# Clamping the chunk sum for the growth factor on ScalarE instead of GpSimd, in a selective state-space block

## The chip, the cores and the metric

The kernel runs on one core of a Trainium2 chip. The metric is the device time of one execution in microseconds (us). Engines are named as in the profile: PE is TensorE's matmul side and PEld its weight loads, DVE is VectorE, ACT is ScalarE, POOL is GpSimd, SP is SyncE, which issues the DMAs.

## The reference, cut to what matters

The input is 8 sequences of 1024 tokens with 512 channels. A layer norm, a Mamba block (1024 inner channels, 16 states per channel, chunks of 128 tokens), a residual, a second layer norm, a product with int8 values and a residual follow one another. The part that the change touches is the scan inside a chunk:

```
A_bar = exp(d_c[..., None] * A)                       # A = -a < 0, one per state
BX = d_c[..., None] * B_c[:, :, None, :] * x_c[..., None]
log_A_cum = cumsum(log(maximum(A_bar, EPS)), axis=1)  # EPS = 1e-10
A_cum = exp(minimum(log_A_cum, 80))
wcum = cumsum(BX / maximum(A_cum_shifted, EPS), axis=1)
h = A_cum * wcum / maximum(A_bar, EPS) + h0 * A_cum
y = einsum('bls,blds->bld', C_c, h) + D * x_c
```

For each state the kernel needs 1 / maximum(A_cum_shifted, EPS), which it calls the growth. With total = the sum of d_c over the earlier tokens of the chunk, the growth is exp(a * min(total, ln(1e10) / a)), which is the same as exp(min(a * total, ln(1e10))).

## The kernel before, in words

A tile is one chunk of 128 tokens (in the partitions) by 1024 channels; there are 64 tiles. For one parity of the tile number two tiles are in flight, so every large buffer of a tile exists twice. The program is written as one instruction stream per engine, by hand: a function `whole` calls for each engine `start`, then `body(tile)` for every tile (a loop over pairs of tiles from tile 4 on, the last pair written out) and `end`. Semaphores that only count up order the engines; every `wait_ge` in the listing is such a wait.

`body` runs over 16 slots, one per state s. In slot s

- PE makes `cum` for slot s+2 (L961: the sum over earlier tokens of `step`, two PSUM buffers), then pieces of the next tile's front (input projection L866, transposes L850, the small projection L879, `total` L895) and of the previous tile's end (transposes L928, output projection L936, int8 product L951), then `state` for slot s (L971: the sum of `source`, one PSUM buffer).
- DVE makes `term` of slot s-1 (L1311: state times decay times C), `source` of slot s+1 (L1298: growth times B times delta times x), adds term s-1 to `acc` (L1321), then its pieces of front and end: the convolution taps (L1159 in slot 5, L1167 in slots 6 and 7), dt (L1191, slot 9), the softplus (L1196, L1201, L1203, slots 10 and 11), `delta` (L1213, slot 12), `dx` (L1222, slot 13), the correction of the last token (L1248, slot 6), the second norm's output `xn` (L1277) with its largest value and scale (L1279 to L1283, slot 15).
- ACT makes `decay` of slot s+2 (L699: exp(-a * cum)) and then `growth` of slot s+2 (L704: exp(a * room), written over `cum` in PSUM), with evacuations of PSUM banks and pieces of the front between them: the small projection `proj` in slot 9 (L568), then in slot 10 abs, exp, relu and ln of the softplus (L631, L635, L637, L641) and one `xc` evacuation, in slot 11 the other `xc` evacuation and the square (L648). At the end of slot 8 it runs two SiLUs (L620, L611) between two table loads (L620, L795). PE's front uses a single PSUM bank, `fbank`, so each front product or transpose waits until ACT has emptied the bank. At the start of slot 0 ACT waits for DVE's scale and quantizes (L685, L687).
- POOL makes `step` of slot s+3 (L463: delta clamped to [0, ln(1e10)/a]; waits until `cum` of slot s+1 is complete, since it has two buffers) and then `room` of slot s+2 (L473: total clamped likewise; one buffer, so it waits for the growth of slot s+1). In slot 14 it also makes `skip` of the next tile (L450: D times x, the start value of `acc`), which waits only for pieces of the front that are done by slot 11.

Slots above 15 belong to the next tile: `step` of the next tile's states 0, 1 and 2 is issued in slots 13, 14 and 15, `room` of its states 0 and 1 in slots 14 and 15. In the source the order of POOL is

```
limit_step(s + 3); limit_sum(s + 2); if s == 0: finish(prev); if s == 14: skip(nxt)
```

and that of ACT in slot 9 to 11 (slot numbers of the scan in brackets)

```
9:  decay(11), proj, growth(11)
10: abs, decay(12), exp, relu, growth(12), xc0, ln
11: decay(13), xc1, square, growth(13)
```

Of the kernel before, what the change touches and what calls it, by code (L numbers as in the profile page):

```python
# [9 lines left out]
ALU = mybir.AluOpType  # L10
ACT = mybir.ActivationFunctionType
AX = mybir.AxisListType

P = 128
BATCH, SEQ, D = 8, 1024, 512
DI = 1024
NS = 16
# [10 lines left out]
FIRST_PARTS = 8  # L28
EPS = 1e-10
LN_EPS = float(np.log(np.float32(EPS)))  # L30
NORM_EPS = 1e-5
INT8_MAX = 127.0
ROUND = 12582912.0
# [18 lines left out]
FRONT_ACT = ("xi0", "xi1", "xiT0", "tap3a", "xiT1", "tap3b", "z0", "xcT", "proj", "abs", "exp", "over", "xc0",  # L52
             "ln", "xc1", "square", "z1", "total0", "total1", "ct")
# [29 lines left out]
def at(steps, tile, name):  # L83

    return tile.n * len(steps) + steps.index(name) + 1


def slot_at(tile, slot):

    return tile.n * NS + slot + 1  # L90
# [7 lines left out]
def before(tile, slot, by):  # L98

    return (tile, slot - by) if slot >= by else (tile.shift(-1), NS - by + slot)  # L100


def mamba_block(nc, x, w_in, conv_w, conv_b, w_x, dt_w, dt_b, a_log, d_skip, w_out, rhs_t, out):
    with ExitStack() as ctx:
        def sb(name, shape, dt=F32):
            return ctx.enter_context(nc.sbuf_tensor(name, shape, dt))
# [4 lines left out]
        def sem(name):  # L111
            return ctx.enter_context(nc.semaphore(name))
# [10 lines left out]
        neg_a = sb("neg_a", [P, NS])  # L123
        pos_a = sb("pos_a", [P, NS])
        limit = sb("limit", [P, NS])
# [9 lines left out]
        rscale = sb("rscale", [P, D])  # L135
        rcol = sb("rcol", [P, KD])
        rinv = sb("rinv", [P, KD])
        curve = sb("curve", [P, 6])
        square_bias, below, above, ln_join, round_up, round_back = (curve[:, i:i + 1] for i in range(6))


        xt = sb("xt", [P, D])
# [18 lines left out]
        total = sb("total", [P, DI])  # L161
# [5 lines left out]
        room = sb("room", [P, DI])  # L167
# [40 lines left out]
        cum = [ps(f"cum{i}", [P, DI]) for i in range(2)]  # L208
# [17 lines left out]
        front_act = sem("front_act")  # L226
# [7 lines left out]
        step_ready = sem("step_ready")  # L234
        room_ready = sem("room_ready")
        cum_ready = sem("cum_ready")
        growth_ready = sem("growth_ready")
# [34 lines left out]
        def stand(eng):  # L272

            eng.sem_inc(stood, 1)
# [139 lines left out]
        def _(pool):  # L414
# [3 lines left out]
            nc.gpsimd.memset(hfirst[:, :], 0.0)  # L418
            nc.gpsimd.memset(last_marks[:, :], 0.0)
            for column, value in ((square_bias, SQUARE_BIAS), (below, -JOIN), (above, 1.0 + JOIN), (ln_join, 0.0),  # L420
                                  (round_up, ROUND), (round_back, -ROUND)):
                nc.gpsimd.memset(column, value)
            for h in halo:
                nc.gpsimd.memset(h[:, :, :], 0.0)
# [38 lines left out]
                nc.gpsimd.tensor_scalar(step[s % 2][:, :], delta[t.parity][:, :], limit[:, s:s + 1], 0.0,  # L463
                                        ALU.min, ALU.max).then_inc(step_ready, 1)

            def limit_sum(t, s):
                if s == 0:
                    pool.wait_ge(front_act, at(FRONT_ACT, t, "total1"))
                user, old = before(t, s, 1)
                if user is not None:  # L470
                    pool.wait_ge(growth_ready, slot_at(user, old))
                stand(pool)
                nc.gpsimd.tensor_scalar(room[:, :], total[:, :], limit[:, s:s + 1], 0.0,  # L473
                                        ALU.min, ALU.max).then_inc(room_ready, 1)

            def finish(t):
                with pool.If(other_carries(pool, t)):
                    a = acc[t.parity][:, :]
                    if isinstance(t.n, int) and t.n == TILES - 1:
                        pool.wait_ge(room_ready, slot_at(t, NS - 1))  # L480
                    else:
                        pool.wait_ge(front_dve, at(FRONT_DVE, t.shift(1), "delta"))
                        pool.wait_ge(room_ready, slot_at(t.shift(1), 2))
                    stand(pool)
                    nc.gpsimd.memset(hcarry, 0.0).then_inc(carry_cleared, 1)
                    pool.wait_ge(carry_cleared, t.n + 1)
                    pool.wait_ge(added, slot_at(t, NS - 1))
                    for s in range(1, NS):
                        pool.wait_ge(carry_terms, carry_at(t, s))
                        if s > 1:  # L490
                            pool.wait_ge(carry_added, carry_at(t, s - 1))
                        stand(pool)
                        nc.gpsimd.tensor_tensor(a, a, carried[:, :], ALU.add).then_inc(carry_added, 1)
                    pool.wait_ge(carry_saved, 16 * carry_at(t))
                    pool.wait_ge(last_saved[0], ring_at(t, NS - 2))
                    pool.wait_ge(last_saved[1], ring_at(t, NS - 1))
                    pool.wait_ge(carry_added, carry_at(t))
                    stand(pool)
                    nc.gpsimd.tensor_tensor(hmain[t.parity], hmain[t.parity], hcarry, ALU.add).then_inc(carry_merged, 1)
                    pool.wait_ge(carry_merged, t.n + 1)  # L500
                with pool.Else():
                    skip_carries(pool, t, carry_added)
                    if not (isinstance(t.n, int) and t.n == 0):
                        pool.wait_ge(carry_merged, t.n)
                    pool.sem_inc(carry_cleared, 1)
                    pool.sem_inc(carry_merged, 1)

            def start():
                t = Tile(0, 0)
                skip(t)  # L510
                for s in range(3):
                    limit_step(t, s)
                for s in range(2):
                    limit_sum(t, s)

            def body(t, more, more2):
                prev, nxt = t.shift(-1), t.shift(1)
                for s in range(NS):
                    if s + 3 < NS:
                        limit_step(t, s + 3)  # L520
                    elif more:
                        limit_step(nxt, s + 3 - NS)
                    if s + 2 < NS:
                        limit_sum(t, s + 2)
                    elif more:
                        limit_sum(nxt, s + 2 - NS)
                    if s == 0 and prev is not None:
                        finish(prev)
                    if more:
                        if s == 14:  # L530
                            skip(nxt)
# [4 lines left out]
        def _(act):  # L536
# [157 lines left out]
            def decays(t, s):  # L694
                act.wait_ge(cum_ready, slot_at(t, s))
                user, old = before(t, s, 4)
                if user is not None:
                    act.wait_ge(term_ready, slot_at(user, old))
                nc.scalar.activation(decay[s % 4][:, :], cum[s % 2][:, :], ACT.Exp, scale=neg_a[:, s:s + 1]).then_inc(decay_ready, 1)  # L699

            def growths(t, s):
                act.wait_ge(decay_ready, slot_at(t, s))
                act.wait_ge(room_ready, slot_at(t, s))
                nc.scalar.activation(cum[s % 2][:, :], room[:, :], ACT.Exp, scale=pos_a[:, s:s + 1]).then_inc(growth_ready, 1)  # L704

            def finish(t):
                with act.If(other_carries(act, t)):
# [6 lines left out]
            def start():  # L714
                t = Tile(0, 0)
                norm_guess(t)
                norm_xnT(t)
                front_xi(t, 0)
                front_xi(t, 1)
                front_xiT(t, 0)  # L720
                front_tap3(t, 0)
                front_xiT(t, 1)
                front_tap3(t, 1)
                front_gate(t, 0)
                front_xcT(t)
                nc.scalar.preload_act_table_set(EXP_AND_LN)
                front_proj(t)
                front_abs(t)
                front_over(t)
                front_xc(t, 0)  # L730
                front_log(t)
                front_xc(t, 1)
                front_square(t)
                front_gate(t, 1)
                front_total(t, 0)
                front_total(t, 1)
                front_ct(t)
                norm_guess(t.shift(1))
                norm_xnT(t.shift(1))
                decay_once(t)  # L740
                for s in range(2):
                    decays(t, s)
                    growths(t, s)

            def body(t, more, more2):
                prev, nxt = t.shift(-1), t.shift(1)
                prev2 = prev.shift(-1) if prev is not None else None
                for s in range(NS):
                    ahead, slot = (t, s + 2) if s + 2 < NS else (nxt, s + 2 - NS)
                    if s == 0 and prev2 is not None:  # L750
                        end_q(prev2)
                    if s == 10 and more:
                        front_abs(nxt)
                    if more or s + 2 < NS:
                        decays(ahead, slot)

                    if s == 0 and prev is not None:
# [333 lines left out]
        def _(dve):  # L1091
# [17 lines left out]
            done(nc.vector.reciprocal(limit[:, :], pos_a[:, :]), limit_ready, 1)  # L1109
            nc.vector.tensor_scalar(limit[:, :], limit[:, :], -LN_EPS, None, ALU.mult).then_inc(limit_ready, 1)  # L1110
            nc.vector.tensor_scalar(neg_a[:, :], pos_a[:, :], -1.0, None, ALU.mult).then_inc(consts_dve, 1)
# [356 lines left out]
```

## Time and profile before

| | |
|---|---|
| runs | 6188.1, 6189.16, 6192.53 us; median 6189.16 us |
| profiled execution | 6189.9 us from its first to its last instruction; the page gives no time outside this span |
| mean granted TensorE clock | 0.989 of full speed |
| PE / DVE / ACT / POOL busy | 92% / 91% / 60% / 44% of the span |
| instructions that the change touches | 1024 `room` on POOL (L473), 1024 `growth` on ACT (L704) |

The busy share of an engine is the union of its instructions over the whole span. The timeline rows give the start in us from the beginning of the span, the duration, the engine, the line in the kernel, the operation, what it writes and reads, and, in square brackets, how long the engine had been idle before it and who ended that idle time. Instructions of one engine overlap a little: the pitch from start to start is shorter than the duration. A row with "x8" stands for eight in a row.

### The profile page before, as it was taken

Reading aid. Unit: us, or ns where it says so; the run is one execution under the profiler, and the core shown is the slowest. Engines: PE = TensorE matmul, PEld = TensorE weight load, DVE = VectorE, ACT = ScalarE, POOL = GpSimd, SP = SyncE. Lnnn points to the kernel's source line nnn. Section 1 sums busy time; section 2 is a strip of 40 time slices with the busy share of each in tenths; the row PEclk is TensorE's granted clock in tenths of the full one; section 3 lists DMA queues with packets and bytes.
Section 4 is the critical chain, followed back from the end, with each engine's and each line's share of the span. In section 5 each row is a group of like instructions: output and inputs, shape, how many; then the busy total and the mean of one; then the engine's idle time right before and its main releaser. Section 6 shows DMA issues by size and latency. Waiting matters only on the chain.

```text
span 6189.9 us, 77161 instructions
## 1 busy us (share of the span) xinstructions
PE 5686.4 (92%) x16152; PEld 2632.6 (43%) x16152; DVE 5633.4 (91%) x7057; ACT 3734.6 (60%) x4618; POOL 2744.1 (44%) x2138
## 2 busy tenths in 40 slices
PE   5999999999999999999999999999999999999997
PEld 2444444444444444444444444444444444444443
DVE  4999999999999999999999999999999999999997
ACT  3666665665666666656666666566566666665664
POOL 2444444444444444444444444444444444444443
PEclk9999999999999999999999999999999999999998
DMA  1121121121111211211212112112121121121120
GB/s 64 11 17 19 14 17 15 14 19 13 16 18 14 17 16 14 19 15 14 19 13 17 16 14 19 15 14 19 13 16 18 14 17 15 14 19 15 14 17 11
DMA packets 157893, 104.23 MB, mean 17 GB/s; under 512 B 121008, under 2 KB 121008, under 8 KB 157488
## 3 DMA queue, kind: packets, MB, share of 16 engines
q1 hardware_dynamic: 157488, 100.71, 17.8%
q14 instruction: 380, 3.11, 0.2%
q8 instruction: 25, 0.41, 0.0%
HBM read 42.63 MB, written 16.78 MB: 10 GB/s over the span
## 4 chain that ended last, share of the span: by engine, by line
PE 37%; DVE 31%; issue 20%; ACT 3%; DVEq 2%; ACTq 0%; DMA 0%; SPq 0%
PE state L971 13%; DVE acc L1321 11%; PE cum L961 10%; DVE term L1311 6%; PE fbank L866 5%; DVE conv L1167 4%; DVE conv L1159 2%; PE ebank L936 2%; PE ebank L916 2%; PE fbank L879 2%; DVE xn L1277 1%; ACT xiT L568 1%; DVE dx L1222 1%; DVE delta L1213 1%; PE fbank L850 1%
## 5 line engine op out<-in xcount | busy, mean ns | idle before, releaser
L699 ACT ACTIVATE decay<-cum,neg_a 128x1024 f32<-128x1024 f32 x1024 | 1138.6, 1112 | 1944.8 <-PE cum L961 1942.4
L971 PE MATMUL state<-sources,tri_upto 128*128 128x512 f32 x4096 | 1980.6, 606 | 187.4 <-DVE term L1311 187.1
L473 POOL TENSOR_SCALAR room<-total,limit 128x1024 f32<-128x1024 f32 x1024 | 1352.8, 1321 | 1653.9 <-ACT cum L704 1448.2
L463 POOL TENSOR_SCALAR step<-delta,limit 128x1024 f32<-128x1024 f32 x1024 | 1243.4, 1214 | 1661.2 <-PE cum L961 1038.5
L961 PE MATMUL cum<-step,tri_before 128*128 128x512 f32 x4096 | 1940.7, 596 | 3.5 <-DVE sources L1298 3.5
L1311 DVE SCALAR_TENSOR_TENSOR term<-state,crow,decay 128x1024 f32<-128x1024 f32 x1024 | 1308.8, 1278 | 247.4 <-PE state L971 135.9
L1321 DVE TENSOR_TENSOR acc<-acc,term 128x1024 f32<-128x1024 f32 x1024 | 1459.2, 1425 | 0.2
L1298 DVE SCALAR_TENSOR_TENSOR sources<-cum,brow,dx 128x1024 f32<-128x1024 f32 x1024 | 1303.1, 1273 | 12.1 <-ACT cum L704 12.1
L971 PEld LDWEIGHTS state<-sources,tri_upto 128*128 128x128 f32 x4096 | 744.5, 191 | 1068.5 <-issue 941.7
L961 PEld LDWEIGHTS cum<-step,tri_before 128*128 128x128 f32 x4096 | 777.7, 192 | 941.7 <-issue 935.6
L704 ACT ACTIVATE cum<-room,pos_a 128x1024 f32<-128x1024 f32 x1024 | 1143.6, 1117 | 17.6 <-POOL room L473 2.7
L866 PE MATMUL fbank<-win,xnT 128*128 128x512 f32 x2048 | 983.3, 603 | 113.4 <-ACT xiT L568 109.4
L866 PEld LDWEIGHTS fbank<-win,xnT 128*128 128x128 f32 x2048 | 376.5, 191 | 573.9 <-issue 423.4
L936 PE MATMUL ebank<-wout,ygT 128*128 128x512 f32 x1024 | 484.0, 596 | 0.5 <-DVE ygT L1248 0.5
L936 PEld LDWEIGHTS ebank<-wout,ygT 128*128 128x128 f32 x1024 | 190.8, 191 | 217.3 <-issue 202.1
L1167 DVE SCALAR_TENSOR_TENSOR conv<-xiT,cw,conv 128x128 f32<-128x128 f32 x1024 | 279.4, 334 | 0.2
L597 ACT ACTIVATE conv<-xiT,cb,cw 128x128 f32<-128x128 f32 x512 | 210.1, 489 | 0.1
L1159 DVE SCALAR_TENSOR_TENSOR conv<-xiT,cw,conv 128x128 f32<-128x128 f32 x512 | 189.7, 440 | 18.3 <-ACT conv L597 18.3
L1201 DVE SCALAR_TENSOR_TENSOR xi<-acc,xi 128x1024 f32<-128x1024 f32 x64 | 78.4, 1225 | 131.4 <-ACT acc L648 131.4
L450 POOL TENSOR_TENSOR acc<-xiT,dskip 128x1024 f32<-128x1024 f32 x64 | 151.9, 2374 | 78.7 <-DVE xi L1201 78.7
L685 ACT ACTIVATE xn<-xn,curve,esmall 128x512 f32<-128x512 f32 x64 | 52.1, 813 | 213.8 <-DVE esmall L1283 213.8
L895 PE MATMUL fbank<-delta,tri_before 128*128 128x512 f32 x256 | 137.3, 618 | 20.8 <-ACT total L568 19.8
(125 smaller groups left out, 3972.7 us busy)
## 6 DMA issues: line engine op xcount, KB each, us to landing
hfirst<-hrows SPq DMA_DIRECT2D x496, 64.0 KB, 3.9
xt<-in_x SPq DMA_DIRECT2D x64, 256.0 KB, 2.6
hrows<-term SPq DMA_DIRECT2D x1024, 4.0 KB, 1.7
xres<-in_x SPq DMA_DIRECT2D x64, 256.0 KB, 2.7
out_x<-xres SPq DMA_DIRECT2D x64, 256.0 KB, 2.1
gate_last<-gate SPq DMA_DIRECT2D x512, 0.5 KB, 2.1
win<-in_w_in SPq DMA_DIRECT2D x2, 2048.0 KB, 10.7
hrows<-hrows SPq DMA_DIRECT2D x64, 64.0 KB, 2.3
```

Of the source, the lines that this page charges most:

```text
L463: nc.gpsimd.tensor_scalar(step[s % 2][:, :], delta[t.parity][:, :], limit[:, s:s + 1], 0.0, ALU.min, ALU.max).then_inc(step_ready, 1)
L473: nc.gpsimd.tensor_scalar(room[:, :], total[:, :], limit[:, s:s + 1], 0.0, ALU.min, ALU.max).then_inc(room_ready, 1)
L699: nc.scalar.activation(decay[s % 4][:, :], cum[s % 2][:, :], ACT.Exp, scale=neg_a[:, s:s + 1]).then_inc(decay_ready, 1)
L704: nc.scalar.activation(cum[s % 2][:, :], room[:, :], ACT.Exp, scale=pos_a[:, s:s + 1]).then_inc(growth_ready, 1)
L866: last = nc.tensor.matmul(fbank[:, :], xnT[t.parity][:, k, :], win[:, k, col:col + HALF], start=(k == 0), stop=(k == KD - 1))
L936: last = nc.tensor.matmul(ebank[:, :], ygT[:, k, :], wout[:, k, :], start=(k == 0), stop=(k == KI - 1))
L961: last = nc.tensor.matmul(cum[s % 2][:, cols], tri_before[:, :], step[s % 2][:, cols], start=True, stop=True)
L971: last = nc.tensor.matmul(state[:, cols], tri_upto[:, :], source[s % 2][:, cols], start=True, stop=True)
L1167: last = nc.vector.scalar_tensor_tensor(out=conv[:, k, :], in0=xiT[:, k, tap:tap + P], scalar=cw[:, k, tap:tap + 1], in1=conv[:, k, :], op ...
L1298: nc.vector.scalar_tensor_tensor(out=source[s % 2], in0=cum[s % 2][:, :], scalar=brow[t.parity][:, s:s + 1], in1=dx[t.parity][:, :], op0=A ...
L1311: nc.vector.scalar_tensor_tensor(out=term[s % 2][:, :], in0=state[:, :], scalar=crow[t.parity][:, s:s + 1], in1=decay[s % 4][:, :], op0=AL ...
L1321: nc.vector.tensor_tensor(sums, sums, term[s % 2][:, :], ALU.add).then_inc(added, 1)
```

## The change

`room` is no longer a clamped sum but the distance to the clamp, relu(ln(1e10) - a * total), and it is made on ACT; the growth is then exp(ln(1e10) - room). The two forms of the growth are equal in exact arithmetic. ACT issues `rooms` right before `decays` of the same slot (in slot 0 after the quantization, in slot 10 after abs); POOL keeps `step` and `skip`. `room` stays a single buffer.

```diff
+LN_TOP = -LN_EPS
...
-        curve = sb("curve", [P, 6])
+        curve = sb("curve", [P, 7])
...
-            def limit_sum(t, s):
-                if s == 0:
-                    pool.wait_ge(front_act, at(FRONT_ACT, t, "total1"))
-                user, old = before(t, s, 1)
-                if user is not None:
-                    pool.wait_ge(growth_ready, slot_at(user, old))
-                stand(pool)
-                nc.gpsimd.tensor_scalar(room[:, :], total[:, :], limit[:, s:s + 1], 0.0,
-                                        ALU.min, ALU.max).then_inc(room_ready, 1)
...
             def finish(t):
...
-                        pool.wait_ge(room_ready, slot_at(t, NS - 1))
+                        pool.wait_ge(step_ready, slot_at(t, NS - 1))
...
-                        pool.wait_ge(room_ready, slot_at(t.shift(1), 2))
+                        pool.wait_ge(step_ready, slot_at(t.shift(1), 3))
...
-                for s in range(2):
-                    limit_sum(t, s)
...
-                    if s + 2 < NS:
-                        limit_sum(t, s + 2)
-                    elif more:
-                        limit_sum(nxt, s + 2 - NS)
...
+            def rooms(t, s):
+
+                if s == 0:
+                    act.wait_ge(front_act, at(FRONT_ACT, t, "total1"))
+                user, old = before(t, s, 1)
+                if user is not None:
+                    act.wait_ge(growth_ready, slot_at(user, old))
+                nc.scalar.activation(room[:, :], total[:, :], ACT.Relu, bias=ln_top, scale=neg_a[:, s:s + 1]).then_inc(room_ready, 1)
+
             def growths(t, s):
+
                 act.wait_ge(decay_ready, slot_at(t, s))
                 act.wait_ge(room_ready, slot_at(t, s))
-                nc.scalar.activation(cum[s % 2][:, :], room[:, :], ACT.Exp, scale=pos_a[:, s:s + 1]).then_inc(growth_ready, 1)
+                nc.scalar.activation(cum[s % 2][:, :], room[:, :], ACT.Exp, bias=ln_top, scale=-1.0).then_inc(growth_ready, 1)
...
                 for s in range(2):
+                    rooms(t, s)
                     decays(t, s)
                     growths(t, s)
...
                     if more or s + 2 < NS:
+                        rooms(ahead, slot)
                         decays(ahead, slot)
```

## Rows read from the trace of the kernel before

**Rows 1.** The page: busy time, share of the span and instructions of each engine.

```profile
PE 5686.4 (92%) x16152; PEld 2632.6 (43%) x16152; DVE 5633.4 (91%) x7057; ACT 3734.6 (60%) x4618; POOL 2744.1 (44%) x2138
```

**Rows 2.** Waits: engine, line, who ended them; total us, times, longest.

```profile
ACT decay L699 <- PE cum L961: 1942.4, 772, 6.8
...
PE state L971 <- DVE term L1311: 187.1, 222, 3.4
```

**Rows 3.** PE's timeline, slots 14 to 0, first tile of a pair.

```profile
3032.15 1.95 PE L971 MATMUL state<-sources,tri_upto 128*128 128x512 f32 x4 [0.45 <-DVE term L1311]
...
3043.97 0.39 PE L945 MATMUL ebank<-ident_bf,q_bf 128*128 128x128 bf16 x4 [0.42 <-ACT q_bf L687]
```

**Rows 4.** DVE's timeline at the end of the next tile, the second of its pair.

```profile
3138.47 1.28 DVE L1311 SCALAR_TENSOR_TENSOR term<-state,crow,decay 128x1024 f32<-128x1024 f32 x1 [3.19 <-ACT decay L699]
```

**Rows 5.** PE's timeline, slots 7 and 8.

```profile
3083.00 1.95 PE L971 MATMUL state<-sources,tri_upto 128*128 128x512 f32 x4 [0.95 <-DVE term L1311]
...
3088.70 1.53 PE L971 MATMUL state<-sources,tri_upto 128*128 128x512 f32 x3 [0.32 <-DVE term L1311]
```

**Rows 6.** ACT's timeline, slots 9 to 11 of one tile.

```profile
3000.57 1.11 ACT L699 ACTIVATE decay<-cum,neg_a 128x1024 f32<-128x1024 f32 x1
3001.58 0.19 ACT L568 ACTIVATE proj<-fbank 128x33 f32<-128x33 f32 x1
...
3003.59 1.06 ACT L631 ACTIVATE xi<-conv 128x1024 f32<-128x1024 f32 x1 [0.75 <-DVE conv L1191]
...
3005.61 1.05 ACT L635 ACTIVATE xi<-xi 128x1024 f32<-128x1024 f32 x1
3006.70 1.15 ACT L637 ACTIVATE over<-xi,curve 128x1024 f32<-128x1024 f32 x1
...
3011.83 1.11 ACT L699 ACTIVATE decay<-cum,neg_a 128x1024 f32<-128x1024 f32 x1 [1.43 <-PE cum L961]
```

**Rows 7.** PE's timeline, slots 10 and 11 of the tile of rows 6.

```profile
3009.42 0.66 PE L850 MATMUL fbank<-ident,xcT 128*128 128x128 f32 x4 [0.98 <-ACT xiT L568]
...
3013.48 1.98 PE L866 MATMUL fbank<-win,xnT 128*128 128x512 f32 x4 [1.69 <-ACT xiT L568]
```

**Rows 8.** DVE's timeline, slots 5 and 6 of the next tile.

```profile
3072.07 2.97 DVE L1159 SCALAR_TENSOR_TENSOR conv<-xiT,cw,conv 128x128 f32<-128x128 f32 x8
...
3078.60 0.96 DVE L1248 TENSOR_TENSOR ygT<-ygT,fix_gated 128x8 f32<-128x8 f32 x1
3079.49 2.17 DVE L1167 SCALAR_TENSOR_TENSOR conv<-xiT,cw,conv 128x128 f32<-128x128 f32 x8
```

**Rows 9.** POOL's timeline, slots 13 and 14.

```profile
3025.15 1.11 POOL L473 TENSOR_SCALAR room<-total,limit 128x1024 f32<-128x1024 f32 x1
3026.23 1.11 POOL L463 TENSOR_SCALAR step<-delta,limit 128x1024 f32<-128x1024 f32 x1
...
3031.70 2.36 POOL L450 TENSOR_TENSOR acc<-xiT,dskip 128x1024 f32<-128x1024 f32 x1
```

**Rows 10.** DVE's timeline, slots 13 to 15.

```profile
3026.68 1.74 DVE L1321 TENSOR_TENSOR acc<-acc,term 128x1024 f32<-128x1024 f32 x1
3028.35 1.21 DVE L1222 TENSOR_TENSOR dx<-delta,xiT 128x1024 f32<-128x1024 f32 x1
...
3033.11 2.03 DVE L1321 TENSOR_TENSOR acc<-acc,term 128x1024 f32<-128x1024 f32 x1
...
3039.80 1.34 DVE L1277 TENSOR_SCALAR xn<-x,emv,esmall 128x512 f32<-128x512 f32 x1
```

**Rows 11.** POOL's timeline, slot 13 of the first tile.

```profile
185.75 2.15 POOL L463 TENSOR_SCALAR step<-delta,limit 128x1024 f32<-128x1024 f32 x1
```

**Rows 12.** DVE's timeline there.

```profile
185.76 1.25 DVE L1321 TENSOR_TENSOR acc<-acc,term 128x1024 f32<-128x1024 f32 x1
186.93 2.05 DVE L1222 TENSOR_TENSOR dx<-delta,xiT 128x1024 f32<-128x1024 f32 x1
```

**Rows 13.** POOL's timeline, beside the second tap of rows 8.

```profile
3080.54 2.10 POOL L463 TENSOR_SCALAR step<-delta,limit 128x1024 f32<-128x1024 f32 x1 [1.00 <-PE cum L961]
```

More of the change, by code:

```diff
@@ L137, in mamba_block @@
         rinv = sb("rinv", [P, KD])
-        curve = sb("curve", [P, 6])
-        square_bias, below, above, ln_join, round_up, round_back = (curve[:, i:i + 1] for i in range(6))
+        curve = sb("curve", [P, 7])
+        square_bias, below, above, ln_join, round_up, round_back, ln_top = (curve[:, i:i + 1] for i in range(7))
         xt = sb("xt", [P, D])
@@ L420, in _ @@
             for column, value in ((square_bias, SQUARE_BIAS), (below, -JOIN), (above, 1.0 + JOIN), (ln_join, 0.0),
-                                  (round_up, ROUND), (round_back, -ROUND)):
+                                  (round_up, ROUND), (round_back, -ROUND), (ln_top, LN_TOP)):
                 nc.gpsimd.memset(column, value)
```

## The prediction

> **What bounds the kernel now.** I read the busy table first, then the waits, then the timelines of two tiles slot by slot. By busy time PE (92%) and DVE (91%) bound together, and ACT and POOL look half free [rows 1]. The waits seem to say that the move is free: ACT stands idle for 1942.4 us in all before a decay until PE has its cum, and 1024 new relus of about 1.2 us would fit into that [rows 2]. But these are sums over stages. Slot by slot there are three kinds of stretch.
>
> Slots 0 to 3 and 11 to 15 are PE's: its instructions follow each other without a gap, apart from 0.45 us before the state of slot 14 and 0.42 us before the int8 transposes in the first tile of a pair of the loop [rows 3]. The second tile has one larger gap: its last term starts after DVE has been idle for 3.19 us, where DVE's loop jumps back (its listing shows nothing else there; the releaser named is an inference) [rows 4].
>
> Slots 4 to 8 are DVE's, but only just: PE waits for DVE's terms of slots 6 and 7, 0.95 and 0.32 us, and for nothing else [rows 5].
>
> Slots 8 to 11 are ACT's. Between the decay of slot 9 and the one of slot 11 ACT is idle for 0.75 us, until dt is there, and then for 1.43 us, until cum(13) is there, which itself had waited for ACT's first xc evacuation [rows 6]. PE stands still for that evacuation (0.98 us) and for the second one (1.69 us) [rows 7]. Ahead of it, in slot 8, two table loads and two SiLUs run back to back.
>
> **The change part by part.**
>
> *The relu itself.* It reads SBUF and takes a per-partition scale and a per-partition bias. No such row exists with both at 1024 columns. Without either the exp of the softplus takes 1.05 us, with a bias alone the relu of the softplus takes 1.15 [rows 6]: a pointer costs 0.1, so I take 1.25, between 1.15 and 1.35. From start to start it is 0.1 less, as for the decay before proj (1.11 long, proj 1.01 later) [rows 6]: 1.15 us in a chain. The growth swaps a scale pointer for a bias pointer: nothing, and at most 0.1 either way. No table load is added: relu already runs between exp and ln of the softplus without one.
>
> *Where it costs.* In 13 of 16 slots ACT is idle before the decay, or reaches it late without anybody waiting; there the relu is covered by the wait for cum. If that cover went, each slot would cost up to 1.15. In slot 9 it stands between a table load and decay(11), and proj is behind that: ACT is busy throughout, so proj, and with it dt on DVE, is 1.15 later. In slot 10 it stands between abs and decay(12); exp, relu, growth(12) and xc0 are behind it: another 1.15. In slot 11 the relu fits into the 1.43 us before decay(13). So the first xc evacuation, PE's transposes, cum(13), the second evacuation and the z product all come 2.3 us later, counted from cum(10); what is late next is PE, whose 0.98 becomes over 3.
>
> *What the removal gives.* `room` collides with DVE instructions that read two SBUF tensors. The first tap takes 2.97 for eight, the second 2.17: 0.8 lost. The correction of 8 columns takes 0.96, where a tap of 128 columns takes 0.27: 0.7 to 0.8 lost [rows 8]. Both lie in DVE's stretch, so DVE gains 1.5 there; PE can follow only by what it waits at slot 7, 0.95, before cum(10) [rows 5]. (Its 0.32 in slot 8 is won too and lost again at xc0.) Other collisions with room, in slots 0 to 3, 7 and 11, lie where PE or ACT ends last: nothing, since PE has no gap there to close. Net for slots 4 to 11: dt moves by 1.15 - 0.95 = 0.2, of which 0.05 is slack, then 1.15: **+1.3 us in each of 63 tiles, 82 us**. Bounds: with a relu of 1.35 and no gain +2.7, with 1.15 and the full 1.27 +0.8.
>
> *What moves.* POOL's order loses room between its instructions, and so skip, which stood behind room of slot 14, is issued right behind step(1). That step no longer waits for room (1.11) [rows 9] but for cum(15), some 0.3 us sooner: about 25.95 to 27.05 on the scale of these rows, and skip, 2.36 us long, is issued at 27.0 instead of 31.70. At that time DVE has acc(12), issued at 26.68 and blocked by the step, and then dx at 28.1, both with two SBUF inputs [rows 10]. In the first tile the same meeting is on record: a step issued beside acc waited for acc (2.15 instead of 1.11), then ran before dx, which took 2.05 instead of 1.21 [rows 10, 11, 12]. So acc ends at 28.1, skip at 30.4, dx at 31.5 instead of 29.56: +1.9. On DVE this is won back in part: acc(13) beside skip took 2.03 against 1.25 [rows 10, 12], and xn 1.34, where half the columns of dx should take 0.6 (an estimate): -0.8 each, so the scale comes 0.3 late. On PE state(14) is 1.9 late; 0.2 of it goes into the wait for the next evacuation and 0.42 into the gap before the int8 transposes [rows 3]: +1.3. In the first tile of a pair PE decides, **+1.3**; in the second DVE's 3.19 [rows 4] still hides PE's part, **+0.3**. For 31 pairs: **50 us**; bounds 0 (skip harmless) and 2 x 1.9 x 31 = 118.
>
> A rule weighed here: the tap rows show the opposite order, a step issued beside the second tap waited 2.10 while taps issued after it went on undisturbed [rows 8, 13]. The Trainium skill ("SBUF — State Buffer", Who interferes with whom) says that of DVE and GpSimd the one that starts first holds the shared pair for its whole instruction. By that rule skip goes ahead of dx and the sum stands; by the tap rows dx would go first, which is the second rival.
>
> *Edits at nothing.* The waits moved from room to step in POOL's finish belong to a branch that the profile does not show taken; the seventh column of curve is one more memset at the start; `start` puts two relus ahead of the first source: 2.3 us once. DMAs: none added or moved, SP passes nothing.
>
> *Sum.* 82 + 50 + 2 = 134 us on the profiled 6189.9 us, which is the span, 0.7 over the median: **6323 us**, 2.2% slower. A measurement of this kernel can tell about 0.2% (12 us) from no change.
>
> **The rivals.**
>
> 1. *Faster: ACT's chain does not decide.* Then the terms of slots 6 and 7 come earlier and PE follows by 0.95 + 0.32 [rows 5]: 63 x 1.27 = 80. If skip does no harm either, the second tile of each pair gains the 0.8 of acc(13) and the 0.8 of xn, and the first 0.4: 2.0 x 31 = 62. 6190 - 142 = **6048**, within the 187.1 that PE waits for terms in all [rows 2]. For it: ACT's idle sum, DVE's share. Against it: ACT's solid work around [rows 6]. It decides if a relu before decay(11) and decay(12) delays by under 0.1 us each, since 2 x 0.1 x 63 + 50 would still be below 80. The same section of the Trainium skill says that ScalarE has its own ports and that a DVE instruction with two SBUF inputs contends only with GpSimd reading; that alone would point here.
> 2. *Skip waits until dx is through.* dx loses nothing, acc(13) and xn are free: -2.0 per pair as above, 82 - 62 + 2 = +22: **6212**. For it [rows 13], against it [rows 11, 12], where the same instructions met.
> 3. *Nothing comes back.* Steps, now always issued as cum ends, take over room's collisions: 63 x 2.3 + 50 + 2 = 197: **6387**. Against it: most steps already start when cum ends.
>
> That the change does not do what it says I exclude: relu needs no other table, and POOL's 1024 instructions are simply gone.
>
> **How the numbers follow.** Forecast 0.50; rival 1 0.25 (spread from 6010 to 6175, depending on skip); rival 2 0.13 (6190 to 6240); rival 3 0.12 (6350 to 6400). A range from **6110 to 6385** leaves out half of rival 1 and half of rival 3, under 2 in 10. The likeliest case alone is 6285 to 6350, by its bounds. Faster by over 0.2%: 0.25; within: 0.08, the near end of rival 2 and of rival 1; slower: 0.67.
>
> **What would show it.** Right: relu near 1.25 us; proj and abs later against cum(10); PE's wait before the transposes of xc from 0.98 to over 3, before the z product near 1.7; the first tap near 2.2 and the correction near 0.2; skip starting 3 to 4 us earlier against cum(0), and dx over 3 us. Step by step wrong: dx still 1.21 (rival 2); no longer waits at xc0 while tiles get shorter (rival 1); taps as long as before (rival 3). The whole forecast is wrong if slots 8 to 11 take no longer than before.

## The result, and the profile after

The changed kernel takes **6456.74 us**, median of four runs (6444.96 to 6468.05), against 6188.65 for the kernel before in the same comparison: ratio **1.0429, 95% interval 1.0413 to 1.0446**. The forecast was 6323 us, slower, with a range up to 6385: the side was right, the size was half of what came (+134 forecast, +268 measured), and the range did not hold it. The profiled execution took 6447.77 us, its span is 6446.0 us, and its mean granted TensorE clock is 0.960, where before it was 0.989.

First the busy table of the changed kernel, then two of its groups (busy us, mean ns of one, idle before):

```profile
PE 5802.4 (90%) x16152; PEld 2706.4 (42%) x16152; DVE 5531.6 (86%) x7057; ACT 4918.8 (76%) x5642; POOL 1415.1 (22%) x1115
...
L693 ACT ACTIVATE room<-total,curve,neg_a 128x1024 f32<-128x1024 f32 x1024 | 1263.5, 1234 | 12.0
...
L1219 DVE TENSOR_TENSOR dx<-delta,xiT 128x1024 f32<-128x1024 f32 x64 | 213.2, 3332 | 0.1
```

Against [rows 1], ACT gained 1184 us of work and POOL lost 1329, as the diff says. One number fits no step of the prediction: PE, which the change does not touch, is busy for 116 us more with the same 16152 instructions, while its mean granted clock fell from 0.989 to 0.960. Where the extra time sits is read below, from matmuls of one shape at either level of the clock.

The waits of the changed kernel (engine, line, who ended them; total us, times, longest):

```profile
ACT decay L684 <- PE cum L958: 974.7, 569, 6.9
...
PE fbank L847 <- ACT xiT L553: 230.6, 65, 4.4
PE state L968 <- DVE term L1308: 208.2, 99, 2.8
```

ACT's idle time before decays has halved against [rows 2]: the relus did fit into the sum. What they cost is in the second row: PE's wait for the xc evacuation (L850 before), 0.98 us in [rows 7].

Slots 9 to 11 of one tile, ACT's timeline of the changed kernel (start, length, ..., idle before and its releaser):

```profile
4511.21 1.24 ACT L693 ACTIVATE room<-total,curve,neg_a 128x1024 f32<-128x1024 f32 x1
4512.35 1.09 ACT L684 ACTIVATE decay<-cum,neg_a 128x1024 f32<-128x1024 f32 x1
4513.35 0.19 ACT L553 ACTIVATE proj<-fbank 128x33 f32<-128x33 f32 x1
...
4515.35 1.06 ACT L616 ACTIVATE xi<-conv 128x1024 f32<-128x1024 f32 x1 [0.75 <-DVE conv L1188]
4516.32 1.23 ACT L693 ACTIVATE room<-total,curve,neg_a 128x1024 f32<-128x1024 f32 x1
...
4521.61 0.57 ACT L553 ACTIVATE xiT<-fbank 128x512 f32<-128x512 f32 x1
```

The relu lasts 1.24 us and moves the decay behind it by 1.14, as forecast. It stands at the two places named: ahead of decay(11), which holds up proj and so dt (the 0.75 of [rows 6] is unchanged, dt's chain simply came later), and behind abs, ahead of decay(12) and xc0's evacuation. The same slots on PE, and below them the same view of another tile:

```profile
4522.24 0.66 PE L847 MATMUL fbank<-ident,xcT 128*128 128x128 f32 x4 [3.58 <-ACT xiT L553]
4522.74 3.14 PE L958 MATMUL cum<-step,tri_before 128*128 128x512 f32 x4
4527.57 1.98 PE L863 MATMUL fbank<-win,xnT 128*128 128x512 f32 x4 [1.69 <-ACT xiT L553]
...
3531.35 1.11 PE L847 MATMUL fbank<-ident,xcT 128*128 128x128 f32 x4 [3.59 <-ACT xiT L553]
3532.25 3.62 PE L958 MATMUL cum<-step,tri_before 128*128 128x512 f32 x4
3537.57 3.78 PE L863 MATMUL fbank<-win,xnT 128*128 128x512 f32 x4 [1.69 <-ACT xiT L553]
3541.14 3.10 PE L933 MATMUL ebank<-wout,ygT 128*128 128x512 f32 x4
```

PE stands (waits with nothing to do) for 3.58 us, 2.6 more than in [rows 7], and 1.69 as before: the forecast said "over 3" and "near 1.7". But cum(13), 1.88 us long elsewhere, now takes 3.14 in the first tile, and in the second everything up to the output projection is slow. The stretches of the first tile (us, busy time of PE, PEld, DVE, ACT, POOL, then PEclk, DMA share, GB/s) say why:

```profile
4514.00:4518.60 4.60, 4.60 (x14) 1.87 (x12) 4.60 (x5) 3.85 (x5) 1.31 (x1) 1.00 0.17 9
4518.60:4522.20 3.60, 0.06 (x1) 0.00 (x0) 2.72 (x7) 3.57 (x5) 0.00 (x0) 1.00 0.27 10
4523.30:4526.60 3.30, 2.58 (x4) 0.49 (x2) 1.61 (x2) 1.74 (x2) 0.52 (x1) 0.50 0.05 2
4527.60:4532.00 4.40, 4.40 (x11) 2.01 (x12) 2.51 (x2) 3.20 (x3) 0.00 (x0) 1.00 0.00 0
```

Before the stand and during it the granted clock is 1.00 (2.4 GHz), after it 0.50 (1.2 GHz), and from 4527.6 on 1.00 again. The low stretch lies on the chain: cum(13) comes later, with it decay(13) and the z product.

DVE's timeline at the taps and, below, at the end of a pair, and then POOL's at the end of the pair:

```profile
4490.86 2.18 DVE L1156 SCALAR_TENSOR_TENSOR conv<-xiT,cw,conv 128x128 f32<-128x128 f32 x8
...
4496.61 0.15 DVE L1245 TENSOR_TENSOR ygT<-ygT,fix_gated 128x8 f32<-128x8 f32 x1
...
4540.77 1.48 DVE L1318 TENSOR_TENSOR acc<-acc,term 128x1024 f32<-128x1024 f32 x1
4542.17 3.37 DVE L1219 TENSOR_TENSOR dx<-delta,xiT 128x1024 f32<-128x1024 f32 x1
...
4555.44 0.54 DVE L1274 TENSOR_SCALAR xn<-x,emv,esmall 128x512 f32<-128x512 f32 x1
```

```profile
4540.06 1.11 POOL L464 TENSOR_SCALAR step<-delta,limit 128x1024 f32<-128x1024 f32 x1 [0.80 <-PE cum L958]
4541.14 3.32 POOL L451 TENSOR_TENSOR acc<-xiT,dskip 128x1024 f32<-128x1024 f32 x1
```

The first tap and the correction are rid of the clamp (2.97 and 0.96 in [rows 8]). Skip is issued right behind the step, waits for acc and goes ahead of dx, which ends 3.37 us after its start, against 1.21 in [rows 10]; xn is back from 1.34 to 0.54.

### The profile page after: what moved, and what is told of

Read it like the earlier page. It is cut to its first block and busy times, and to the rows that moved or that the text cites. A ratio compares the mean times of both kernels' runs of the same rounds, so it can differ in the third digit from the quotient of the medians.

```text
span 6446.0 us, 76230 instructions
## 1 busy us (share of the span) xinstructions
PE 5802.4 (90%) x16152; PEld 2706.4 (42%) x16152; DVE 5531.6 (86%) x7057; ACT 4918.8 (76%) x5642; POOL 1415.1 (22%) x1115
## 5 line engine op out<-in xcount | busy, mean ns | idle before, releaser
L464 POOL TENSOR_SCALAR step<-delta,limit 128x1024 f32<-128x1024 f32 x1024 | 1200.2, 1172 | 4894.6 <-PE cum L958 3828.3
L958 PE MATMUL cum<-step,tri_before 128*128 128x512 f32 x4096 | 2022.4, 618 | 2.1 <-DVE sources L1295 2.1
L1318 DVE TENSOR_TENSOR acc<-acc,term 128x1024 f32<-128x1024 f32 x1024 | 1358.3, 1326 | 0.2
L693 ACT ACTIVATE room<-total,curve,neg_a 128x1024 f32<-128x1024 f32 x1024 | 1263.5, 1234 | 12.0
L699 ACT ACTIVATE cum<-room,curve 128x1024 f32<-128x1024 f32 x1024 | 1143.1, 1116 | 14.9
L863 PE MATMUL fbank<-win,xnT 128*128 128x512 f32 x2048 | 1018.1, 621 | 112.6 <-ACT xiT L553 109.5
L863 PEld LDWEIGHTS fbank<-win,xnT 128*128 128x128 f32 x2048 | 387.1, 197 | 617.7 <-issue 436.5
L847 PE MATMUL fbank<-ident,xcT 128*128 128x128 f32 x512 | 95.2, 317 | 230.2 <-ACT xiT L553 229.9
L1164 DVE SCALAR_TENSOR_TENSOR conv<-xiT,cw,conv 128x128 f32<-128x128 f32 x1024 | 277.9, 333 | 0.2
L451 POOL TENSOR_TENSOR acc<-xiT,dskip 128x1024 f32<-128x1024 f32 x64 | 212.2, 3316 | 78.6 <-DVE xi L1198 78.6
L1219 DVE TENSOR_TENSOR dx<-delta,xiT 128x1024 f32<-128x1024 f32 x64 | 213.2, 3332 | 0.1
L847 PEld LDWEIGHTS fbank<-ident,xcT 128*128 128x128 f32 x512 | 67.6, 158 | 316.1 <-ACT xiT L553 282.5
```

The lines of the kernel that those rows point to most:

```text
L693: nc.scalar.activation(room[:, :], total[:, :], ACT.Relu, bias=ln_top, scale=neg_a[:, s:s + 1]).then_inc(room_ready, 1)
L863: last = nc.tensor.matmul(fbank[:, :], xnT[t.parity][:, k, :], win[:, k, col:col + HALF], start=(k == 0), stop=(k == KD - 1))
L958: last = nc.tensor.matmul(cum[s % 2][:, cols], tri_before[:, :], step[s % 2][:, cols], start=True, stop=True)
L1164: last = nc.vector.scalar_tensor_tensor(out=conv[:, k, :], in0=xiT[:, k, tap:tap + P], scalar=cw[:, k, tap:tap + 1], in1=conv[:, k, :], op ...
L1318: nc.vector.tensor_tensor(sums, sums, term[s % 2][:, :], ALU.add).then_inc(added, 1)
```

## The experiments

The letters are those of the expectations. **A**: the forecast's mechanism (ACT's longer chain in slots 8 to 11, skip ahead of dx), and on top a third term, the clock that falls after PE's longer stand. **B**: simply the sum of ACT's work, 1024 relus alike. **C**: the clock falls for another reason than the stand. A fourth was weighed as well: the forecast's mechanism alone, with its sizes misjudged. The kernel before took 6191.5 to 6192.6 us in the experiments' comparisons. Where a slot's length is given, it is the time from its term's start on DVE to the next term's, mean of tiles 10 to 59.

### Each part undone

One kernel gives back to GpSimd the two clamps of slots 11 and 12, the ones that stood in the way (ACT issues them in its slots 9 and 10; `limit_sum` is the old function, issued as before):

```diff
+ON_POOL = (11, 12)
...
                         limit_step(nxt, s + 3 - NS)
+                    if s + 2 in ON_POOL:
+                        limit_sum(t, s + 2)
...
-                nc.scalar.activation(cum[s % 2][:, :], room[:, :], ACT.Exp, bias=ln_top, scale=-1.0).then_inc(growth_ready, 1)
+                form = {"scale": pos_a[:, s:s + 1]} if s in ON_POOL else {"bias": ln_top, "scale": -1.0}
+                nc.scalar.activation(cum[s % 2][:, :], room[:, :], ACT.Exp, **form).then_inc(growth_ready, 1)
...
-                        rooms(ahead, slot)
+                        if slot not in ON_POOL:
+                            rooms(ahead, slot)
                         decays(ahead, slot)
```

> The changed kernel with the clamped sums of slots 11 and 12 back on GpSimd (14 of 16 stay on ScalarE). Theory A (two relus in ScalarE's slots 9 and 10 lengthen its chain by 2.2 us per tile, and PE's longer stand before the xc transposes drops its clock right after): chain -2.2 x 63 = -140, clock -70 to -90, so 6457 - 220 = about 6235 (6215 to 6260), and the low stretches of the clock near slot 11 are gone. Rival B (it is the sum of ScalarE's work, 1024 relus alike): two sixteenths of the loss come back, 33 us: about 6424. Rival C (the clock falls for another reason): 6317, low stretches as before.

Measured: **6157.51 us**, ratio 0.9944 [0.9927, 0.996] to the kernel before. In tiles 2 to 61 no stretch at 0.50 begins in slots 9 and 10 any more, where the changed kernel has 57; that speaks against rival C.

Another lets skip wait until dx is done:

```diff
-                pool.wait_ge(front_dve, at(FRONT_DVE, t, "poly"))
+                pool.wait_ge(front_dve, at(FRONT_DVE, t, "dx"))
```

> The changed kernel with skip waiting until dx is done. Theory A: dx falls from 3.3 to 1.2 us, term(13) follows 2 us earlier, the low stretches of the clock around slots 13 and 14 go; 50 us directly and 20 to 40 by the clock: 6457 - 80 = about 6375 (6355 to 6400). Rival (skip's collision is hidden by PE): 6457 +- 12.

Measured: **6330.35 us**, ratio 1.0227 [1.021, 1.0244]. The third has both edits:

> Both edits together: clamped sums 11 and 12 on GpSimd, skip after dx. Theory A: nothing of the loss is left and the taps, the correction and xn stay free of GpSimd: 6189 less 0.95 to 1.3 us in each of 63 tiles and up to 1 us in every second one, about 6100 (6070 to 6150). Rival B (sum of ScalarE's work): about 6350. If the gain of the taps is worth nothing: 6189 +- 15.

Measured: **6016.92 us**, ratio 0.9717 [0.9701, 0.9733], clock 0.995. This beats both kernels by a wide margin and is called the best version below. Its pair's end, POOL's timeline and then DVE's:

```profile
4235.13 2.36 POOL L452 TENSOR_TENSOR acc<-xiT,dskip 128x1024 f32<-128x1024 f32 x1 [2.40 <-DVE dx L1233]
```

```profile
4233.73 1.21 DVE L1233 TENSOR_TENSOR dx<-delta,xiT 128x1024 f32<-128x1024 f32 x1
```

All three runs came out below their expected ranges, by 25 to 58 us: theory A had the directions right and the sizes too small. So two of sixteen clamps and the place of one instruction decide between -2.8% and +4.3%. Skip's place is worth 126 us with all relus on ACT (6456.74 - 6330.35) and 141 without the two (6157.51 - 6016.92). The two relus are worth 313 us (6330.35 - 6016.92), or five us per tile, twice what their 2 x 1.15 can explain. That is where the forecast fell short.

### The clock, with the chain left as it is

To tell A from C and from the mechanism alone, PE gets work in its long stand that delays nothing: it makes cum(13) once more, unsignalled, ahead of the transposes it waits for. The proper cum(13) follows at its old place and overwrites it; all else is as in the changed kernel.

```diff
                         if s == 10:
+                            pe.wait_ge(step_ready, slot_at(t, 13))
+                            pe.wait_ge(source_ready, slot_at(t, 11))
+                            for h in range(2):
+                                cols = slice(h * HALF, (h + 1) * HALF)
+                                nc.tensor.matmul(cum[1][:, cols], tri_before[:, :], step[1][:, cols], start=True, stop=True)
                             front_xc(nxt, 1)
```

> The changed kernel where PE, while it stands still at the end of slot 10, makes cum(13) once more without telling anybody (1.7 us of work into 3.6 us of idle time), and then everything as before. Nothing waits for it, so only the clock can answer. Theory A (the clock falls because PE stood still): low stretches near slot 11 mostly gone, 1.0 to 1.4 us per tile back: about 6380 (6365 to 6410). Rival C (the clock falls for another reason): 6457 +- 15, low stretches as before.

Measured: **6348.71 us**, ratio 1.0249 [1.0232, 1.0266]: 252 more matmuls, and 108 us faster than the changed kernel; that is 16 us below the expected range. PE's timeline, and the windows of the stand and of what follows:

```profile
4440.83 1.88 PE L1070 MATMUL cum<-step,tri_before 128*128 128x512 f32 x4
4444.57 0.66 PE L847 MATMUL fbank<-ident,xcT 128*128 128x128 f32 x4 [1.86 <-ACT xiT L553]
4445.06 1.88 PE L958 MATMUL cum<-step,tri_before 128*128 128x512 f32 x4
4448.63 1.98 PE L863 MATMUL fbank<-win,xnT 128*128 128x512 f32 x4 [1.69 <-ACT xiT L553]
```

```profile
4441.00:4444.60 3.60, 1.74 (x5) 0.43 (x4) 2.73 (x7) 3.57 (x5) 0.00 (x0) 1.00 0.24 9
4445.70:4449.00 3.30, 1.61 (x4) 0.49 (x3) 1.53 (x2) 3.00 (x4) 1.12 (x1) 1.00 0.07 7
```

The transposes still come as late, but the clock stays at 1.00, and cum(13) takes 1.88 again. In this kernel the clock still falls in slot 13 of some tiles, where PE stands for the late dx; so the same edit was made with skip behind dx:

> The changed kernel with skip after dx, and PE making cum(13) once more while it stands still in slot 10. What is left of the loss is ScalarE's chain alone, without the clock: the run with both edits (6017) plus 2.25 us in 63 tiles = about 6160 (6145 to 6185), no low stretch in slots 9 to 11. If the clock had not been the cause, 6330 as with the late skip alone.

Measured: **6181.74 us**, ratio 0.9983 [0.9974, 0.9993], clock 0.995. Against 6330.35 that is **149 us that only the clock can have given back**: nothing waits for the added matmuls, and the granted clock of the profiled executions goes from 0.963 to 0.995. Slot 10 shows it: 10.5 to 10.6 us in each of 60 tiles (2 to 61) here; with skip late and no extra matmuls it is 10.6 in 3 of them, 11.9 to 12.7 in 32, and 14.1 to 15.8 in 25. And against the 6016.92 of the kernel without the two relus, **165 us** are left at a clock that holds. The chain accounts for 142 of them: 2.25 us per tile in slots 8 to 10 (23.86 against 21.6 us). The rest stands mostly in slot 0 of every second tile (4.13 against 3.52) and is a cost of the extra matmuls themselves: with skip late and without them this slot takes 3.52 as well. In about half of the pairs PE waits there, and no other engine is named as the end of the wait (PEq is PE's sequencer, "issue" a wait for nothing that the profile shows; with skip late and no extra matmuls neither row occurs):

```profile
PE fbank L863 <- PEq L271: 23.0, 15, 2.0
...
PE cum L958 <- issue: 19.8, 14, 1.8
```

So 149 us is the least that the clock cost, and by 313 - 142 it was some 170.

Does cum(13) ahead of the transposes, once and for good, help?

```diff
-                    if s + 2 < NS:
+                    if more and s == 11:
+                        pass
+                    elif s + 2 < NS:
                         cumulate(t, s + 2)
...
                         if s == 10:
+                            cumulate(t, 13)
                             front_xc(nxt, 1)
```

> The changed kernel with cum(13) made on PE ahead of the second xc transposes, not behind them. Theory A: ScalarE's chain no longer waits 1.5 us for cum(13), PE's longest stand is cut to under 2 us and its clock holds: (1.5 + 1.2) x 63 = 170 back, about 6287 (6265 to 6330). Rival C (clock falls for another reason): 6457 - 95 = 6362.

Measured: **6384.03 us**, ratio 1.0313 [1.0295, 1.033], clock 0.968: better than the changed kernel by 73 us, worse than the repetition, and a miss: by its time alone rival C's 6362 would fit better than the 6265 to 6330 of theory A. The trace speaks for A even so. The work that filled the first stand is missing from behind it, and the second wait grows: PE's wait before L863 goes from 109.5 to 191.7 us in all. In each of 63 tiles the granted clock falls during that wait or within 0.3 us of its end, and the z product behind it is slow (1.98 in [rows 7]):

```profile
4472.09 3.61 PE L863 MATMUL fbank<-win,xnT 128*128 128x512 f32 x4 [2.99 <-ACT xiT L553]
```

### The kernel before, made worse

The kernel before with an idle relu (it reads `total` and writes a spare bf16 buffer that nobody reads) ahead of the decays issued in slots 9 and 10:

```diff
                     if more or s + 2 < NS:
+                        if s in (9, 10):
...
+                            nc.scalar.activation(spare[:, :], total[:, :], ACT.Relu, bias=above, scale=neg_a[:, slot:slot + 1])
                         decays(ahead, slot)
```

> The kernel before, GpSimd's work untouched, with one more relu of 128x1024 on ScalarE in slot 9 and in slot 10, ahead of the decay, into a spare bf16 buffer that nobody reads. Theory A: +2.2 us in 63 tiles (140) and 60 to 90 for the clock: 6189 + 210 = about 6400 (6370 to 6430). Rival B (sum of ScalarE's work): two sixteenths of 268, about 6222.

Measured: **6504.83 us**, ratio 1.0497 [1.048, 1.0515], clock 0.953, 75 us above the expected range. PE's timeline:

```profile
4561.65 0.66 PE L855 MATMUL fbank<-ident,xcT 128*128 128x128 f32 x4 [3.17 <-ACT xiT L569]
4562.14 3.58 PE L966 MATMUL cum<-step,tri_before 128*128 128x512 f32 x4
```

The same relu in the other fourteen slots (`s not in (9, 10)`):

> The kernel before with the same relu in the 14 other slots and none in slots 9 and 10. Theory A: hidden by the waits for cum, 6189 to 6220. Rival B: fourteen sixteenths of 268, about 6424.

Measured: **6226.27 us**, ratio 1.0057 [1.004, 1.0073]. 128 relus in two slots cost 313 us, the 313 found above (that it is the same to the microsecond is luck, since the two kernels differ elsewhere); seven times as many in the other slots cost 35, a little more than expected. The sum of ACT's work (rival B) is not the cause. Skip's place in the kernel before, first ahead of the clamp, as it came to stand by the change:

```diff
+                    if s == 14 and more:
+                        skip(nxt)
                     if s + 2 < NS:
                         limit_sum(t, s + 2)
...
-                    if more:
-                        if s == 14:
-                            skip(nxt)
```

> The kernel before with skip issued ahead of the clamped sum in slot 14 (right behind step(1)), nothing else changed. Theory A: dx is blocked to over 3 us; 50 us directly and 0 to 40 by the clock: about 6255 (6230 to 6285). Rival (PE hides it): 6189 +- 12.

Measured: **6308.21 us**, ratio 1.0188 [1.0171, 1.0205], clock 0.984: +117, 23 us above the expected range. DVE's timeline shows the dx of the changed kernel:

```profile
4452.44 3.36 DVE L1221 TENSOR_TENSOR dx<-delta,xiT 128x1024 f32<-128x1024 f32 x1
```

And skip behind dx in the kernel before, by the one-line diff above:

> The kernel before, clamped sums all on GpSimd, with skip waiting until dx is done: does the gain of the run with both edits (175 us against the kernel before) come from skip's place and not from the move? Skip already ran behind dx, so theory A expects 6189 +- 12; the rival, that skip's collision with acc(13) cost time in the kernel before, expects up to 50 us less.

Measured: **6191.33 us**, ratio 0.9999 [0.999, 1.0009]. There the clamp holds skip back anyway; so none of the gain of the best version is skip's place by itself.

### Two tries at a better version, both misses

Only the clamps of slots 2, 8 and 9 on ACT, that of 13 and the rest on GpSimd, skip behind dx (`ON_POOL` is all slots but these three):

> Only the clamped sums of slots 2, 8 and 9 on ScalarE, the 13 others on GpSimd, skip after dx. Theory: the gain of the move lies in the three collisions with xn, the first tap and the correction, so three relus in slots where ScalarE waits give most of it: about 6030 (6005 to 6060). Rival (every clamped sum that leaves GpSimd helps DVE): about 6150.

Measured: **6095.63 us**, ratio 0.9845 [0.9828, 0.9861], clock 0.988. The tap slots came out as hoped, but the clamps left on GpSimd still collide late in the tile: slots 12 and 13 take 11.6 us together where the best version takes 10.5, and slot 15 of a pair's second tile 7.0 instead of 6.2, with the clock lower on the mean.

Then the best version with cum(13) early:

> Clamped sums 11 and 12 on GpSimd, skip after dx, and cum(13) made ahead of the second xc transposes. ScalarE no longer waits 1.4 us for cum(13) and PE's stand of 1 us goes: -1.0 to -1.4 us in 63 tiles, about 5945 (5925 to 5965). If DVE takes over as the bound there: 6017 +- 12.

Measured: **6074.99 us**, ratio 0.9813 [0.9797, 0.9829], clock 0.980, 58 us slower than the best version. PE's timeline of the best version first, then of this one:

```profile
4215.06 0.66 PE L861 MATMUL fbank<-ident,xcT 128*128 128x128 f32 x4 [1.33 <-ACT xiT L565]
...
4219.13 1.98 PE L877 MATMUL fbank<-win,xnT 128*128 128x512 f32 x4 [1.69 <-ACT xiT L565]
```

```profile
4161.37 1.88 PE L972 MATMUL cum<-step,tri_before 128*128 128x512 f32 x4
...
4166.52 3.17 PE L877 MATMUL fbank<-win,xnT 128*128 128x512 f32 x4 [2.83 <-ACT xiT L565]
4169.48 2.44 PE L947 MATMUL ebank<-wout,ygT 128*128 128x512 f32 x4
```

PE stands 0.2 us less in all, but in one piece of 2.83 us instead of 1.33 and 1.69, and the z product behind it takes 3.17 instead of 1.98. In 50 of 63 tiles the clock falls at this stand; in the best version it falls in none of the tiles 1 to 61. This is the clock of theory A once more, which the expectation had forgotten.

## Why the prediction was right on the side and wrong on the size

**What failed** is the net of slots 4 to 11, "+1.3 us in each of 63 tiles, 82 us", and in it the sentence "what is late next is PE, whose 0.98 becomes over 3". The step stopped there: PE's stand was taken as the end of the cost, and the matmuls behind it were priced at the length they had before, that is, a fall of the clock was put at nothing without a reason. The runs put it at 149 us at the least. The sum by terms, measured as differences of runs and, in the second and third row, of slots:

| term | forecast | measured |
|---|---|---|
| ACT's chain in slots 8 to 11, with the start | 63 x 2.3 + 2 = 147 | 6182 - 6017 = 165, of it 142 in slots 8 to 10 |
| taps and correction free of the clamp | -63 x 0.95 = -60 | -80 |
| pair's end: skip ahead of dx, less acc and xn | +50 | +126 - 95 = +31 |
| clock after PE's stand in slot 10 | not priced | 6330 - 6182 = +149, at the least |
| sum | +134 (terms rounded, 0.05 of slack per tile taken off) | +265 |

The -80 and -95 divide the 175 us by which the best version beats the kernel before, by its slots, summed over all tiles of the two traces: slots 4 to 10 are 81 us shorter, 1.27 per tile (129 us won in slots 4, 5 and 7, 56 given back in slot 8), and slots 12 to 14 are 96 us shorter, 3.1 per pair. That the rows add up to 265, close to the +268 of the comparison, proves nothing: made as they are, they must add up to the difference of the two kernels. What the runs show is how it divides. Without the fourth row it is +116, and +93 if the extra matmuls' own 23 us are moved from the first row to the fourth: the other three terms together were forecast some 20 to 40 us too high, and the fourth was missing. Two things were not separated: the 126 of skip's place holds low stretches of the clock behind the late dx, and the 95 holds those at the ends of pairs, which the kernel before has and the best version has not.

**Could the trace of before have shown it?** Yes, in rows that the prediction did not read. These are PE's timeline at the ends of two pairs, and the windows over what follows:

```profile
2949.43 3.14 PE L971 MATMUL state<-sources,tri_upto 128*128 128x512 f32 x4 [2.42 <-DVE term L1311]
...
3139.81 1.98 PE L971 MATMUL state<-sources,tri_upto 128*128 128x512 f32 x4 [2.40 <-DVE term L1311]
```

```profile
2950.20:2953.40 3.20, 3.20 (x5) 1.18 (x4) 3.06 (x4) 0.00 (x0) 0.09 (x1) 0.50 0.10 15
3140.90:3144.20 3.30, 3.30 (x9) 1.39 (x8) 3.16 (x4) 0.57 (x1) 0.49 (x1) 1.00 0.14 24
```

PE stands 2.4 us in both, where DVE's loop jumps back by the forecast's reading; after one the clock is 0.50 and a state takes 3.14 us, after the other 1.00 and 1.98. Of 28 such stands of 2.3 to 2.6 us a low stretch goes with 17. So a stand of this length can already cost a low stretch in which one group of four matmuls loses 1.2 us, and a forecast that lengthens a stand from 0.98 to over 3 us in every tile needed this term. By these rows it lies between 0 and 1.2 us or more per tile, 63 x 1.2 = 76 us; the measured 149 is twice that, so the rows show that the term is there and not its full size.

**What was right**, step by step:
- *The relu*: 1.25 us long and 1.15 in a chain forecast, 1.234 and 1.14 measured. No cost for the growth's swapped pointer: 1.12 long.
- *Where it costs*: in slots 9 and 10 nearly alone; fourteen others together cost 35 us in the kernel before. PE's two waits came out as forecast.
- *What the removal gives*: the first tap forecast near 2.2 for eight, the correction near 0.2; measured 2.18 and 0.15. PE could use 1.27 us of this per tile, the 0.95 and the 0.32 of [rows 5], not the 0.95 alone: a small error on the careful side.
- *Skip ahead of dx*: forecast that acc goes first, then skip, then dx, 3.4 us from dx's issue to its end; measured 3.37. Of [rows 11, 12] and [rows 13] it is the first kind that decides. The rule of the Trainium skill ("SBUF — State Buffer", Who interferes with whom), that of DVE and GpSimd the one that starts first holds the shared pair for its whole instruction, agrees here: skip held it, and the 3.32 us of its row are its own 2.36 and about 1.0 of waiting for acc. By that rule alone [rows 13] stay unexplained, and no run here was made for them. The forecast read them as a wait of 2.10 us; that is the row's whole length, 1.11 of it the step's own [rows 9], so the step waited about 1.0.
- *Back at acc and xn*: forecast 2.0 us per pair, measured 3.1 in slots 12 to 14; as skip's own damage was larger too (126 us against 50 + 62 = 112), the net is 31 for 50.

**The rivals.** The first, faster because ACT's chain does not decide, at 6048 us, is what the best version comes close to, at 6017; its condition, a delay under 0.1 us per relu, is met only with the two clamps back on GpSimd. The second needed dx unharmed: made by hand that is 6330, not 6212; without the clock's 149 it is 6182, the case that the extra matmuls show. The third, nothing won back, came nearest in time (6387) but for the wrong reason: the taps did come free.

## What to carry to other kernels

An idle sum on an engine says nothing of the few places where a chain runs through it without a gap: two of sixteen moved instructions cost 313 us, the others next to nothing, so move the others and leave these two. When an edit lengthens a stand of TensorE, price what runs behind it at both levels of the granted clock, and look in the trace of before which stands it is at 0.50 behind, and how often. And when an instruction is taken out of an in-order queue, look at what then starts earlier: one wait, behind dx instead of in front of it, was worth 126 us.

## What the runs showed of the hardware that was not expected

- The clock falls after stands that look harmless in a kernel whose PE is busy for over 90% of the span: of 63 stands of 2.83 us, 50 went with a stretch at 0.50; two of 1.33 and 1.69 us with 2.4 us of matmuls between did in none of the tiles 1 to 61; and of 28 stands of 2.3 to 2.6 us, 17 did. With the stand of 3.6 us slot 10 lost nothing in 3 of 60 tiles, about 1.3 to 2.2 us in 32, and 3.5 to 5.3 in 25. What separates these cases was not tried.
- Useless matmuls can make a kernel faster: 252 of them, 1.88 us per tile in a stand of 3.6, gave 149 us, net of what they cost themselves.
- A relu with a scale and a bias pointer on ACT takes 1.234 us on 128x1024, the exp of the growth with one pointer 1.12, the exp and relu of the softplus 1.04 and 1.15: about 0.1 us per pointer operand.
